# One core: x loaded turned for the router, and all condition matrices by one gather, turned by TensorE

## Chip, cores and metric

The kernel runs on one core of a Trainium2 chip. The metric is the device time of one execution in microseconds (us); the time before is the median of three runs.

## What is computed

x has 32 samples of 64 channels and 512 columns. Each sample is multiplied by one of 200 condition matrices (64 x 64), chosen by its index; the result has 2,048 tokens of 512. A router takes the softmax over 8 experts, and each token's best two. Each expert takes at most 640 assignments in order of tokens (CAP), and the outputs, weighted by the gates, are added to x.

```python
w = weights[conditions]
xc = jnp.einsum('bct,bcd->bdt', x, w)
logits = jnp.einsum('nh,eh->ne', xf, Wr)
gate = jax.nn.softmax(logits, axis=-1)
top2_val, top2_idx = jax.lax.top_k(gate, 2)
rank = (jnp.cumsum(onehot, axis=0) * onehot).sum(-1)
keep = rank <= cap
out_e = jnp.einsum('eni,ehi->enh', silu(g) * u, Wd)
y = jnp.einsum('ne,enh->nh', comb, out_e)
x = x + y
```

## The kernel before

Rows of x, 2,048 of 512, make 16 tiles of 128 rows (two samples each), handled as 8 pairs. The work is written out by hand for each engine, and semaphores order it. It has a front, which conditions and routes, and then the eight experts one after another.

**Router.** The router does not wait for the conditioned rows: it multiplies x by Wr first, and the small product by the condition matrix afterwards. For that TensorE turns each tile of x (x_tile_turn, L1169, four 128x128 turns into a bank of PSUM), ACT or DVE copies it to turned_sb (L600, L810), router(m) (L1180) multiplies, DVE copies the result to xrT (L817), turn(m) (L1193) turns it back and DVE sums it (L823). logits(g) (L1208) multiplies the pairs of group g by their matrices wq; top_two(g) (L826) takes the best two of each token. The groups LG are pairs 0 to 2, 3 and 4, 5 and 6, and 7.

**Condition matrices.** POOL gathers them by index (L446 to L456): for the first eight tiles by eight gathers of 64 rows for each sample straight to wq; for the last eight by one gather of rows of 2,048 bytes to wsel_sb, from which SP places them by eight transfers (place, L359).

**Conditioning.** condition(j) (L1225) multiplies a pair of tiles in eight matrix products of 64x64 by 512, in two rings of two banks; ACT copies each tile to xf_sb (xf_copy, L589) and SP writes each pair to xf_dram (L388 to L394).

**Routing.** From the one-hot matrix (L840) TensorE counts ranks (L1267), DVE works out the slots (L901 to L935) and TensorE puts them into lists (the slot matmuls, L1281), from which DVE makes src_row and dst_row (L950 to L966). TensorE then runs KEEP_WARM matmuls whose result nobody reads (L1287).

**Experts.** POOL gathers tiles of tokens from xf_dram by src_row (gather, L493); the first gather waits for src_row and for all of xf_dram (L484, L485). Weights are loaded by units: four of gate and up, one (KH) of down; for the three-product precision scheme, ACT rounds each unit to a high part (w_high, L604) and DVE takes the rest (w0_low, L937, for expert 0). Once the first gather has landed SP loads expert 1's units (L399 to L402), and, once five tiles have, copies x to out (L405 to L410), for which POOL waits at L568.

The steps on SP that order the front:

```python
            for m in range(NM - 1):
                sp.wait_ge(xf_ok, m * 2 + 2)
                sp.dma_start(xf_t[:, m * 2:m * 2 + 2, :],
                             xf_sb[:, m * 2:m * 2 + 2, :]).then_inc(xf_out, 16)
...
            sp.wait_ge(xg_in[0], 16)
            for u in range(NU):
                sp.wait_ge(wlo0_ok, u + 1)
                load_unit(1, u)
```

## Time and profile before

| what | value |
|---|---|
| runs | 274.13 us median (273.28 to 274.32) |
| the profiled execution | 271.69 us |
| its span, first to last instruction | 270.0 us |
| mean granted clock of TensorE | 0.99 |
| TensorE, DVE, ACT, POOL busy | 257.5, 161.8, 137.6, 171.2 us |
| moved by DMA | 59.00 MB, mean 219 GB/s |

A busy share is a mean over stages with different limits. The front ends at 41.62 us, when TensorE turns the first gathered tile of tokens; from there to the end TensorE has no long gaps. In the rows further down, L12 is line 12 of the kernel; a name with <- is the tile written and those read; xN counts instructions that are merged into one row.

### The profile page before, as it was taken

What the parts mean: (1) busy time and instruction counts of PE and PEld (TensorE: products, weight loads), DVE (VectorE), ACT (ScalarE), POOL (GpSimd) and SP (SyncE); (2) the same over time, 40 slices, a digit from 0 to 9 for tenths busy, and PEclk for the clock granted to TensorE, in tenths of its full rate; (3) what the DMA queues carried; (4) which work ended last, traced back from release to release, by engine and by line L of the source; (5) the groups of instructions that cost most, each with busy time, mean ns of one, the idle gap of its engine ahead of it and who ended that gap; (6) DMA issues with size and microseconds to landing.
All of it is one profiled execution on the core that took longest, in us unless ns stands there. A gap on an engine that the chain in (4) does not pass through costs nothing.

```text
span 270.0 us, 4016 instructions
## 1 busy us (share of the span) xinstructions
PE 257.5 (95%) x1368; PEld 199.9 (74%) x1368; DVE 161.8 (60%) x332; ACT 137.6 (51%) x242; POOL 171.2 (63%) x156
## 2 busy tenths in 40 slices
PE   8999798999999999999999999999999999999991
PEld 4563257999987867888878877887878777778980
DVE  2558997544459674776556638656773967243251
ACT  2356861444464655665376644666475368442100
POOL 5792047731158858875788387768876885585742
PEclk9999979999999999999999999999999999999998
DMA  6999848998879997899789867997899799366541
GB/s 203 364 305 342 358 165 266 382 330 312 298 221 214 203 253 197 138 253 276 178 143 231 245 189 124 241 322 174 171 266 298 127 182 216 41 79 81 146 164 45
DMA packets 27099, 59.00 MB, mean 219 GB/s; under 512 B 6198, under 2 KB 6454, under 8 KB 26976
## 3 DMA queue, kind: packets, MB, share of 16 engines
q1 hardware_dynamic: 16416, 37.89, 44.3%
q0 software_dynamic: 10656, 20.75, 37.2%
q8 instruction: 16, 0.26, 0.4%
q14 instruction: 11, 0.09, 0.1%
HBM read 39.56 MB, written 20.25 MB: 222 GB/s over the span
## 4 chain that ended last, share of the span: by engine, by line
PE 55%; DVE 18%; DMA 9%; ACT 8%; issue 6%; SPq 1%; ACTq 1%; POOLq 0%; DVEq 0%
PE bank L1340 16%; PE bank L1427 10%; PE bank L1314 10%; DMA xg<-xf_dram,src_turn 6%; PE bank L1435 5%; DVE w L996 4%; DVE squares L1045 4%; ACT hhi L695 3%; DMA x_sb<-x 3%; PE bank L1287 2%; PE bank L1301 2%; PE bank L1176 2%; DVE xlo L981 2%; ACT w L608 2%; DVE h L1111 1%
## 5 line engine op out<-in xcount | busy, mean ns | idle before, releaser
L1427 PE MATMUL bank<-xhi,w 128*128 128x512 f32 x280 | 71.5, 397 | 0.2 <-DVE h_last L1091 0.2
L1340 PE MATMUL bank<-w,hhi 128*128 128x512 f32 (+1 forms) x216 | 67.1, 392 | 1.1 <-DVE hlo L1051 1.1
L553 POOL DMA_INDIRECT out<-y_sb,dst_row x35 | 56.1, 1604 | 14.8 <-issue 10.4
L1427 PEld LDWEIGHTS bank<-xhi,w 128*128 128x128 f32 x280 | 52.5, 188 | 13.2 <-DVE h_last L1091 0.7
L519 POOL DMA_INDIRECT gate_g<-gates_dram,src_row x40 | 45.2, 1130 | 12.1 <-issue 10.5
L1340 PEld LDWEIGHTS bank<-w,hhi 128*128 128x128 f32 x216 | 39.2, 188 | 10.2 <-DVE hlo L1051 2.3
L996 DVE TENSOR_TENSOR w<-raw,w 128x704 fp32r<-128x704 f32 (+1 forms) x35 | 37.0, 1058 | 14.6 <-ACT w L608 8.2
L1340 PE MATMUL bank<-w,hlo 128*128 128x512 f32 (+1 forms) x108 | 42.0, 389 | 0.0
L507 POOL DMA_INDIRECT xg<-xf_dram,src_turn x24 | 25.5, 1063 | 26.1 <-DVE xlo L981 11.7
L1435 PE MATMUL bank<-xlo,w 128*128 128x512 f32 x140 | 38.4, 396 | 0.0
L608 ACT ACTIVATE w<-raw 128x704 fp32r<-128x704 f32 (+1 forms) x40 | 36.7, 922 | 0.0
L507 POOL DMA_INDIRECT xg<-xf_dram,src_row x16 | 17.6, 1102 | 27.9 <-DVE dst_row L965 15.7
L1045 DVE STREAM_TRANSPOSE squares<-xg 128x512 f32<-128x512 f32 x24 | 24.0, 1051 | 16.7 <-DMA xg<-xf_dram,src_turn 16.7
L1435 PEld LDWEIGHTS bank<-xlo,w 128*128 128x128 f32 x140 | 26.4, 188 | 6.4
L666 ACT ACTIVATE y_sb<-bank,gate_g 128x512 f32<-128x512 f32 x30 | 20.1, 685 | 20.0 <-PE bank L1340 18.7
L1340 PEld LDWEIGHTS bank<-w,hlo 128*128 128x128 f32 x108 | 20.3, 188 | 4.7
L1314 PE MATMUL bank<-w,xhi 128*128 128x352 f32 x112 | 20.5, 328 | 0.8 <-ACT xhi L643 0.8
L1314 PEld LDWEIGHTS bank<-w,xhi 128*128 128x128 f32 x112 | 18.2, 189 | 1.5 <-issue 1.0
L695 ACT ACTIVATE hhi<-h 128x512 fp32r<-128x512 f32 x14 | 8.8, 632 | 19.5 <-DVE h L1098 12.0
L1051 DVE TENSOR_TENSOR hlo<-h,hhi 128x512 fp32r<-128x512 f32 x14 | 9.7, 696 | 10.4 <-ACT hhi L695 10.4
L981 DVE TENSOR_TENSOR xlo<-xg,xhi 128x512 fp32r<-128x512 f32 x24 | 15.0, 685 | 0.2 <-ACT xhi L653 0.2
L653 ACT ACTIVATE xhi<-xg 128x512 fp32r<-128x512 f32 x24 | 13.2, 617 | 1.5 <-DMA xg<-squares 1.5
(138 smaller groups left out, 304.3 us busy)
## 6 DMA issues: line engine op xcount, KB each, us to landing
raw<-wgu SPq DMA_DIRECT2D x32, 352.0 KB, 7.7
xg<-squares SPq DMA_DIRECT2D x24, 256.0 KB, 7.1
x_sb<-x SPq DMA_DIRECT2D x8, 512.0 KB, 8.3
raw<-wd SPq DMA_DIRECT2D x8, 512.0 KB
xf_dram<-xf_sb SPq DMA_DIRECT2D x7, 512.0 KB, 3.7
raw<-wd SPq DMA_DIRECT2D x8, 192.0 KB
out<-x SPq DMA_DIRECT2D x1, 1280.0 KB, 17.9
gate_g<-gates_dram,src_row POOLq DMA_INDIRECT x40, 4.5
```

The lines of the kernel that those rows point to most:

```text
L507: nc.gpsimd.indirect_dma_start(out=xg[:, t, :], out_offset=None, in_=xf_dram[:, :], in_offset=bass.IndirectOffsetOnAxis(ap=rows, axis=0), ...
L519: nc.gpsimd.indirect_dma_start(out=gate_g[:, n % TPE, :], out_offset=None, in_=gates_dram[:, :], in_offset=bass.IndirectOffsetOnAxis(ap=sr ...
L553: nc.gpsimd.indirect_dma_start(out=out[:, :], in_=y_sb[:, n % TPE, :], in_offset=None, out_offset=bass.IndirectOffsetOnAxis(ap=dst_row[:, ...
L608: last = nc.scalar.activation(w[:, half, 0, a:b], raw[:, a:b], ACT.Copy)
L666: nc.scalar.activation(y_sb[:, t, :], y_bank(e, t)[:, :], ACT.Copy, scale=gate_g[:, t, e:e + 1]).then_inc(y_ok, n)
L981: nc.vector.tensor_tensor(xlo4[:, :, cols], turned_rows(e, t), xhi4[:, :, cols].bitcast(F32), ALU.subtract).then_inc(xlo_ok, n)
L996: last = nc.vector.tensor_tensor(w[:, half, 1, a:b], raw[:, a:b], w[:, half, 0, a:b].bitcast(F32), ALU.subtract)
L1045: nc.vector.transpose(squares[:, :, t, :], xg[:, t, :].rearrange("p (i b) -> p b i", i=SQ)).then_inc(squares_ok, 1)
L1314: last = nc.tensor.matmul(ps[:, 0:I], left[:, b, c], w[:, half, part, o:o + I], start=(k == 0 and left is xhi and part == 0), stop=(k == K ...
L1340: last = nc.tensor.matmul(ps[:, cols], left(c), w[:, half, part, o:o + width], start=(c == 0 and q == 0), stop=(closes and c == cs[-1] and ...
L1427: last = nc.tensor.matmul(ACC_BANK[what][:, :], columns(what, k, part), xhi4[:, k, :], start=(k == 0 and part == 0), stop=False)
L1435: last = nc.tensor.matmul(ACC_BANK[what][:, :], columns(what, k, 0), xlo4[:, k, :], start=False, stop=(k == KH - 1))
```

## The change

x comes from the host a second time, turned within each tile (xt), and is loaded in that form into x_sb, so that router(m) reads it straight from there and no tile is turned before the router. The conditioning still needs rows: for pairs 0 to 2 SP loads them over the turned ones once the router has read those (load_x_rows); for pairs 3 to 7 TensorE turns them back (turn_rows) and ACT copies them over the turned ones (rows_copy). The condition matrices come by one gather for all 32 samples: four partitions for each sample, 17 windows of 64 numbers (4,352 bytes) in each; TensorE turns overlapping pairs of windows (turn_matrices, ahead of router 4), and ACT and DVE copy them from four banks into wq. Conditions run in the order of CONDITIONED.

With it, three weight units of expert 0 are loaded ahead of the writes of xf_dram, the fourth behind them, and the down weights once the first gather has landed; their conversions move behind the conditioning, that of the down weights into the first expert. Exponentials and gates are taken once for all tiles. KEEP_WARM goes from 18 to 24. Below, removed lines are mostly left off; the functions above have them.

```diff
-PLACED = B // 2
-CQ = P // PLACED
-CP = C // CQ
+CQ = P // B
+DP = D // CQ
+WINDOWS = DP + 1
...
-BEFORE_RANKS = 4
-W0_EARLY = 1
+W0_EARLY = 3
+ROWS_LOADED = (0, 1, 2)
+ROWS_TURNED = (3, 4, 5, 6, 7)
+CONDITIONED = (3, 4, 0, 1, 2, 5, 6, 7)
...
-KEEP_WARM = 18
+KEEP_WARM = 24
...
+            def load_x_turned(m):
+                sp.dma_start(x_sb[:, m * 2:m * 2 + 2, :], xt[m, :, :, :]).then_inc(x_in[m], 16)
+            def load_x_rows(n):
+                m = ROWS_LOADED[n]
                 js = slice(m * 2, m * 2 + 2)
+                sp.wait_ge(xrT_ps, m + 1)
+                sp.dma_start(x_sb[:, js, :], x_t[:, js, :]).then_inc(rows_in[n], 16)
             sp.dma_start(condb[:, :], cond[:, :]).then_inc(cond_in, 16)
+            load_x_turned(0)
             sp.dma_start(wr_sb[:, :, :], wr[:, :, :]).then_inc(wr_in, 16)
+            for m in range(1, NM):
...
+                load_x_turned(m)
...
+            for n in range(len(ROWS_LOADED)):
+                load_x_rows(n)
...
+            for u in range(W0_EARLY):
                 load_unit(0, u)
+            for n, m in enumerate(CONDITIONED):
+                sp.wait_ge(xf_ok, n * 2 + 2)
                 sp.dma_start(xf_t[:, m * 2:m * 2 + 2, :],
                              xf_sb[:, m * 2:m * 2 + 2, :]).then_inc(xf_out, 16)
+            for u in range(W0_EARLY, KH):
+                load_unit(0, u)
+            sp.wait_ge(gates_ok, 1)
             sp.dma_start(gates_dram[0:N, :].rearrange("(p j) e -> p j e", j=TT),
                          gate[:, :, :]).then_inc(gates_out, 16)
             sp.wait_ge(xg_in[0], 16)
+            load_unit(0, KH)
...
-            for j in range(HALF):
-                nc.gpsimd.indirect_dma_start(
-                    out=wq[:, j, :], out_offset=None, in_=wcond[:, :],
-                    in_offset=bass.IndirectOffsetOnAxis(ap=cidx[:, j:j + 1], axis=0),
-                ).then_inc(row_in[group_of(j)], 16)
...
+            for b in range(XR):
+                act.wait_ge(wq_ps, b + 1)
+                nc.scalar.activation(wq_view(EVEN, b * XR, XR),
+                                     turned_matrices(b, EVEN, 0, 0, XR),
+                                     ACT.Copy).then_inc(wq_act_ok, 1)
+            def xf_copy(m, ring):
+                act.wait_ge(xf_ps, CONDITIONED.index(m) + 1)
+                for o in range(2):
+                    nc.scalar.activation(xf_sb[:, m * 2 + o, :], ps_xf[ring * 2 + o][:, :],
+                                         ACT.Copy).then_inc(xf_ok, 1)
+            def rows_copy(m, ring):
+                for o in range(2):
+                    act.wait_ge(turned_ps, ROWS_TURNED.index(m) * 2 + o + 1)
+                    nc.scalar.activation(x_sb[:, m * 2 + o, :], ps_xf[ring * 2 + o][:, :],
+                                         ACT.Copy).then_inc(turned_ok, 1)
...
+            rows_copy(3, 0)
+            rows_copy(4, 1)
+            xf_copy(3, 0)
+            xf_copy(4, 1)
+            rows_copy(5, 0)
+            rows_copy(6, 1)
+            xf_copy(0, 0)
+            xf_copy(1, 1)
+            rows_copy(7, 0)
+            xf_copy(2, 1)
+            xf_copy(5, 0)
+            xf_copy(6, 1)
+            xf_copy(7, 0)
+            exps()
...
+                if s == 0:
+                    w_high(KH, 0, 0)
...
+                if m == 4:
+                    for b in range(XR):
+                        dve.wait_ge(wq_ps, b + 1)
+                        n = XR if b < XR - 1 else XR - 1
+                        last = nc.vector.tensor_copy(wq_view(ODD, b * XR + 1, n),
+                                                     turned_matrices(b, ODD, 1, 0, n))
...
+                xrT_copy(m)
                 if m >= 1:
+                    xr_sum(m - 1)
+                if m in (5, 6):
+                    top_two(m - 5)
...
+            def turn_rows(m, ring):
+                for o in range(2):
+                    for k in range(KH):
+                        last = nc.tensor.transpose(ps_xf[ring * 2 + o][:, k * P:(k + 1) * P],
+                                                   xt_sb[:, m * 2 + o, k, :], ident[:, :])
+                    last.then_inc(turned_ps, 1)
...
+            def turn_matrices():
+                pe.wait_ge(wsel_in, 16)
+                for a in range(DP):
+                    last = nc.tensor.transpose(
+                        ps_xf[a // XR][:, a % XR * P:(a % XR + 1) * P],
+                        wsel_sb[:, a * C:(a + 2) * C],
+                        ident[:, :])
+                    if a % XR == XR - 1:
+                        last.then_inc(wq_ps, 1)
...
+                if m in ROWS_LOADED:
+                    pe.wait_ge(rows_in[ROWS_LOADED.index(m)], 16)
+                else:
+                    pe.wait_ge(turned_ok, ROWS_TURNED.index(m) * 2 + 2)
...
+            pe.wait_ge(wr_in, 16)
             for m in range(NM):
+                if m == 4:
+                    turn_matrices()
+                router(m)
                 if m >= 1:
+                    turn(m - 1)
+                if m == 5:
+                    pe.wait_ge(wq_act_ok, XR)
+                    pe.wait_ge(wq_dve_ok, XR)
+                    logits(0)
+                if m == 6:
+                    logits(1)
+                    turn_rows(3, 0)
+            turn_rows(4, 1)
             turn(NM - 1)
             logits(2)
             logits(3)
+            pe.wait_ge(turned_ok, 2)
+            condition(3, 0)
+            pe.wait_ge(turned_ok, 4)
+            condition(4, 1)
+            pe.wait_ge(xf_ok, 2)
+            turn_rows(5, 0)
+            pe.wait_ge(xf_ok, 4)
+            turn_rows(6, 1)
...
+            pe.wait_ge(turned_ok, 6)
+            condition(0, 0)
+            pe.wait_ge(turned_ok, 8)
+            condition(1, 1)
+            pe.wait_ge(xf_ok, 6)
+            turn_rows(7, 0)
+            pe.wait_ge(xf_ok, 8)
+            condition(2, 1)
+            pe.wait_ge(turned_ok, 10)
+            condition(5, 0)
+            pe.wait_ge(xf_ok, 10)
+            condition(6, 1)
+            pe.wait_ge(xf_ok, 12)
+            condition(7, 0)
...
+        "xt": np.asarray(x).reshape(NM, 2, P, KH, P).transpose(0, 4, 1, 3, 2).reshape(NM, P, 2, H),
...
+        "wcond": np.pad(np.asarray(L0_cond_weights).transpose(0, 2, 1).reshape(S * CQ, DP * C),
+                        ((0, 0), (0, C)), mode="wrap"),
```

Where the change moves instructions, these are the places that the prediction speaks of.

ACT, from its first copy on, before (turned_sb is the turned x, xf_sb the conditioned rows, w the rounded weights):

```order
L600 ACTIVATE turned_sb<-bank 128x512 [waits tT_ps] x2
L600 ACTIVATE turned_sb<-bank 128x512 [waits xrT_ps,tT_ps] x9
L592 ACTIVATE xf_sb<-bank 128x512 [waits xf_ps] x2
L619 ACTIVATE ex<-lg 128x80 [waits sub_ok]
L592 ACTIVATE xf_sb<-bank 128x512 [waits xf_ps] x2
L608 ACTIVATE w<-raw 128x704 [waits raw_in0]
L592 ACTIVATE xf_sb<-bank 128x512 [waits xf_ps] x2
L619 ACTIVATE ex<-lg 128x48 [waits sub_ok]
L592 ACTIVATE xf_sb<-bank 128x512 [waits xf_ps] x2
```

and now (wq are the condition matrices, x_sb the rows turned back):

```order
L592 ACTIVATE wq<-bank 64x64x4 [waits wq_ps] x4
L607 ACTIVATE x_sb<-bank 128x512 [waits turned_ps] x4
L600 ACTIVATE xf_sb<-bank 128x512 [waits xf_ps]
L600 ACTIVATE xf_sb<-bank 128x512
L600 ACTIVATE xf_sb<-bank 128x512 [waits xf_ps]
L600 ACTIVATE xf_sb<-bank 128x512
L607 ACTIVATE x_sb<-bank 128x512 [waits turned_ps] x4
L600 ACTIVATE xf_sb<-bank 128x512 [waits xf_ps]
L600 ACTIVATE xf_sb<-bank 128x512
L600 ACTIVATE xf_sb<-bank 128x512 [waits xf_ps]
L600 ACTIVATE xf_sb<-bank 128x512
L607 ACTIVATE x_sb<-bank 128x512 [waits turned_ps] x2
```

Eleven copies of turned x have gone from ahead of the conditioned rows; copies of rows, ten in all, now stand among them, and the weights and exponentials have moved behind.

TensorE around the middle of the router's pairs, before (L1176 turns x, L1188 is the router, L1199 turns its result):

```order
L1188 MATMUL bank_7<-turned_sb,wr_sb 32x256 [waits xrT_ok,tT_act_ok,tT_dve_ok]
L1188 MATMUL bank_7<-turned_sb,wr_sb 32x256 x3
L1199 MATMUL bank_7<-ident,xrT 128x128 [waits xr_ok,xrT_ok]
L1199 MATMUL bank_7<-ident,xrT 128x128
L1176 MATMUL bank<-ident,x_sb 128x128 [waits tT_dve_ok,x_in5]
L1176 MATMUL bank<-ident,x_sb 128x128 x3
L1176 MATMUL bank<-ident,x_sb 128x128 [waits tT_act_ok,x_in5]
L1176 MATMUL bank<-ident,x_sb 128x128 x3
```

and now (L1201 turns the condition matrices, L1157 is the router, L1177 turns its result):

```order
L1177 MATMUL bank_7<-ident,xrT 128x128 [waits xr_ok,xrT_ok]
L1177 MATMUL bank_7<-ident,xrT 128x128
L1201 MATMUL bank<-ident,xf_sb 128x128 [waits wsel_in]
L1201 MATMUL bank<-ident,xf_sb 128x128 x15
L1157 MATMUL bank_7<-x_sb,wr_sb 32x256 [waits xrT_ok,x_in4]
L1157 MATMUL bank_7<-x_sb,wr_sb 32x256 x3
L1177 MATMUL bank_7<-ident,xrT 128x128 [waits xr_ok,xrT_ok]
L1177 MATMUL bank_7<-ident,xrT 128x128
L1157 MATMUL bank_7<-x_sb,wr_sb 32x256 [waits xrT_ok,x_in5]
```

The turns of x ahead of each router are gone, and all turns of matrices stand in one place ahead of router 4, behind a wait for the one gather.

TensorE around the ranks, before (L1232 is the conditioning, L1267 and L1270 the ranks):

```order
L1232 MATMUL bank<-x_sb,wq 64x512 [waits xf_ok]
L1232 MATMUL bank<-x_sb,wq 64x512 x3
L1232 MATMUL bank<-x_sb,wq 64x512 [waits xf_ok]
L1232 MATMUL bank<-x_sb,wq 64x512 x3
L1267 MATMUL bank_7<-ohp,ones 128x264 [waits oh_clear,oh_ok,consts]
L1270 MATMUL bank_7<-ohp,upper 128x128
L1270 MATMUL bank_7<-ohp,upper_odd 128x128
L1232 MATMUL bank<-x_sb,wq 64x512 [waits xf_ok]
L1232 MATMUL bank<-x_sb,wq 64x512 x3
L1232 MATMUL bank<-x_sb,wq 64x512 [waits xf_ok]
L1232 MATMUL bank<-x_sb,wq 64x512 x3
L1232 MATMUL bank<-x_sb,wq 64x512 [waits xf_ok]
```

and now (L1217 is the conditioning, L1167 turns rows back, L1257 and L1260 the ranks):

```order
L1217 MATMUL bank<-x_sb,wq 64x512 [waits turned_ok]
L1217 MATMUL bank<-x_sb,wq 64x512 x3
L1217 MATMUL bank<-x_sb,wq 64x512 [waits turned_ok]
L1217 MATMUL bank<-x_sb,wq 64x512 x3
L1167 MATMUL bank<-ident,x_sb 128x128 [waits xf_ok]
L1167 MATMUL bank<-ident,x_sb 128x128 x7
L1167 MATMUL bank<-ident,x_sb 128x128 [waits xf_ok]
L1167 MATMUL bank<-ident,x_sb 128x128 x7
L1257 MATMUL bank_7<-ohp,ones 128x264 [waits oh_clear,oh_ok,consts]
L1260 MATMUL bank_7<-ohp,upper 128x128
L1260 MATMUL bank_7<-ohp,upper_odd 128x128
L1217 MATMUL bank<-x_sb,wq 64x512 [waits rows_in0,turned_ok]
```

Turns of two pairs, each behind a wait for ACT's copies, have come between the first conditions and the ranks.

## Rows read from the trace of the kernel before

**Rows 1.** The chain of waits, 10 to 45 us (start us, us, what)
```profile
3.22 7.35 DMA x_sb<-x
...
12.65 0.87 PE bank L1176 x8
13.52 0.57 PE bank L1188 x8
14.09 0.37 PE bank L1199 x2
...
33.43 2.55 PE bank L1281 x32
35.98 5.58 PE bank L1287 x18
...
41.62 0.64 PE bank L1301 x4
```

**Rows 2.** ACT in order of time, 31 to 50 us (start, busy, instructions [idle before])
```profile
31.11 2.06 ACT L592 ACTIVATE xf_sb<-bank 128x512 f32 x4 [0.32 <-PE bank L1232]
...
36.64 1.47 ACT L608 ACTIVATE w<-raw 128x1536 fp32r<-128x1536 f32 x1
...
47.61 0.46 ACT L677 ACTIVATE g_sb<-bank 128x352 f32<-128x352 f32 x1 [1.25 <-PE bank L1314]
49.88 0.49 ACT L683 ACTIVATE hhi<-bank 128x384 fp32r<-128x384 f32 x1 [1.80 <-PE bank L1368]
```

**Rows 3.** SP's transfers: the last writes of xf_dram, and the first placing one
```profile
10.87 5.14 SPq L361 DMA_DIRECT2D wq<-xf_sb  x8
...
32.71 1.32 SPq L394 DMA_DIRECT2D xf_dram<-xf_sb  x2
```

**Rows 4.** Transfers issued at 32.0 to 32.6 us (size, us from issue to landing)
```profile
xf_dram<-xf_sb SPq DMA_DIRECT2D x1, 512.0 KB, 3.2
```

**Rows 5.** The same, issued at 33.1 to 34 us
```profile
xf_dram<-xf_sb SPq DMA_DIRECT2D x1, 256.0 KB, 3.5
```

**Rows 6.** POOL in order of time: first gather of matrices, first gather of tokens
```profile
3.38 1.14 POOL L446 DMA_INDIRECT xf_sb<-wcond,cidx  x1 [1.72 <-DVE cidx L792]
...
37.46 1.55 POOL L507 DMA_INDIRECT xg<-xf_dram,src_row  x1 [15.70 <-DVE dst_row L965]
```

**Rows 7.** Transfer queues in 8 to 9 us (packets, MB, share of 16 engines)
```profile
q0 software_dynamic: 21, 0.09, 23.6%
```

**Rows 8.** DVE in order of time, 14 to 20 us
```profile
15.97 0.42 DVE L817 COPY xrT<-bank 128x256 f32<-128x256 f32 x1 [1.25 <-PE bank L1188]
...
18.61 0.54 DVE L831 MAX8 v<-bank 128x8 f32<-128x8 f32 x6 [0.27 <-PE bank L1221]
...
19.96 0.16 DVE L834 FIND_INDEX8 i<-v,bank 128x8 uint32<-128x8 f32 x1
```

**Rows 9.** PE in order of time, 18 to 32 us
```profile
18.01 0.53 PE L1221 MATMUL bank<-xr,wq 64*64 64x8 f32 x24
...
20.69 1.07 PE L1232 MATMUL bank<-x_sb,wq 64*64 64x512 f32 x8
...
27.05 0.27 PE L1267 MATMUL bank<-ohp,ones 128*128 128x264 bf16 x1 [0.49 <-issue]
...
29.86 2.07 PE L1232 MATMUL bank<-x_sb,wq 64*64 64x512 f32 x16 [0.44 <-ACT xf_sb L592]
```

**Rows 10.** Stretches: busy us (instructions) of PE, PEld, DVE, ACT, POOL; PEclk, DMA share, GB/s
```profile
4.00:12.00 8.00, 7.45 (x63) 4.57 (x60) 3.57 (x7) 2.05 (x4) 6.17 (x7) 1.00 1.01 353
32.00:36.00 4.00, 2.57 (x33) 2.52 (x34) 3.96 (x7) 3.98 (x7) 0.00 (x0) 1.00 1.00 392
36.00:39.00 3.00, 3.00 (x8) 1.03 (x7) 2.88 (x11) 2.10 (x3) 1.54 (x1) 0.50 0.10 25
```

**Rows 11.** POOL in order of time: the gathers behind the initial copy to out
```profile
72.41 1.00 POOL L507 DMA_INDIRECT xg<-xf_dram,src_turn  x1 [6.88 <-DMA out<-x]
76.07 1.00 POOL L507 DMA_INDIRECT xg<-xf_dram,src_turn  x1 [2.66 <-PE bank L1301]
```

More of the change, by code:

```diff
@@ L271, in build @@
         xf_t = xf_dram[0:N, :].rearrange("(p j) h -> p j h", j=TT)
-        TURN_DVE = [1, 2, 5, 6, 9]
-        TURN_ACT = [j for j in range(TT) if j not in TURN_DVE]
         def group_of(j):
@@ L1272, in _ @@
             last.then_inc(rank_ps, 1)
-            for j in range(after, TT, 2):
-                condition(j)
+            pe.wait_ge(turned_ok, 6)
[12 more added lines that the diff above has]
+            condition(7, 0)
             pe.wait_ge(consts, CONSTS)
```

222 lines of the change are left out of this document (61 added, 161 removed).

## The prediction

> **What bounds the kernel now.** I read the chain of waits first, then each engine in order of time up to 45 us, then the transfers, and last the places further on where a moved transfer could be late. From 41.62 us on the chain is TensorE at work on the first expert; the change touches little behind that point. So the question is when the first gathered tile of tokens can be turned, 41.62 now [rows 1]. Two things end just there: 18 warming matmuls end at 41.56 [rows 1], and the first gather, issued at 37.46 [rows 6], lands. The gather waits for the token list and for all writes of xf_dram. The slot matmuls that make the list end at 33.43 + 2.55 = 35.98 [rows 1]. ACT's last copy of conditioned rows ends at 31.11 + 2.06 = 33.17 [rows 2]; the last write is the second of a pair of issues that begins at 32.71 and takes 1.32, so issued at about 33.2 [rows 3], and lands 3.5 later, at 36.7 [rows 5]. That is later than the list, and the gather's start follows it by 0.76. The row names dst_row, for which this gather does not wait; the writes were what came last. **The bound of this stage is therefore: ACT's copies, the last write, the gather.** A write of a whole pair, issued half a microsecond before, took 3.2 [rows 4], as long as a half: no queue of transfers stood in front of them. They wait for ACT.
>
> **What is removed.** 64 TensorE turns of x, 0.87 us for each pair [rows 1], and their 16 copies on ACT and DVE go from ahead of the router. Eight small gathers on POOL and eight placing transfers go too. None of that is a gain by itself: the router needs x, and pair 3 lands at 3.22 + 7.35 = 10.57 [rows 1]; transfer engines stand at a share of 1.01 from 4 to 12 us [rows 10]. The cover of the removed work, the arrival of x, stays.
>
> **What is added ahead of the logits: one gather that all of them wait for.** Now the gather is issued from 3.38 to 4.52 [rows 6], has 0.09 MB moved in 8 to 9 us [rows 7], and the first placing transfer, which waits for it, starts at 10.87 [rows 3]. It moves 128 rows of 2,048 bytes, 0.26 MB; the new one moves 128 rows of 17 x 64 x 4 = 4,352 bytes, 0.56 MB. Lower bound 10.8 (size is hidden), upper bound 15 (it comes behind all of x). I take 11.5: nearest is today's gather, and 0.30 MB more at 392 GB/s [rows 10] is 0.75. The Trainium skill, "DMA: Bandwidth & Descriptors", section "Queues, rings and completion order", has each transfer engine take turns between queues, a packet at a time; by that the gather would wait for one pair of x at most, and its landing would lie at the lower bound, 0.7 us less in the sum. The 0.09 MB that it moved in 8 to 9 us beside x [rows 7] agree with the turns; that it is still at work 3.5 us after its issue ended does not.
>
> In order from 11.5: 16 turns of matrices at 0.87 / 8 = 0.109 [rows 1], 13.3; router of pair 4, 0.57 [rows 1]; DVE's last matrix copy and the copy of the router's result, each as the 256-column copy, 0.42 [rows 8], 14.5; router of pair 5, 0.57, 15.0; a turn, 0.37 [rows 1], 15.4; the first logits, 0.5 [rows 9], 15.9. Then DVE's first top two, 18.61 to 20.12 now, 1.5 [rows 8]: 17.6 with hand-overs. The second logits wait for it, and TensorE's first rows to be turned back stand behind those: **18.0**. x is not later: pair 4 would need 0.5 MB more than pair 3, at 353 GB/s [rows 10] 1.5 us, and the new gather's 0.56 MB another 1.6, so 13.7 at worst against the 13.3 at which its router is wanted; I take nothing for it.
>
> **What is added behind: ten more copies on ACT, in one line with the sixteen it has.** Turning back five pairs gives TensorE 40 turns, 4.4 us, and ACT 10 copies. ACT then has 26 copies of 512 columns; four take 2.06 now [rows 2], 0.49 each behind one another: 12.7. The first can start 0.6 after its turns do (four at 0.109 and the hand-over). In two rings of two banks each copy also frees the bank of TensorE's next step, so the two engines take turns. A condition takes TensorE 1.07 [rows 9], and today's copies start 31.11 - 29.86 = 1.25 behind a start of conditions [rows 2, 9]. Written out step by step this leaves ACT idle five times: 0.85 while TensorE runs router 7 and a turn ahead of the next rows; 1.4 while it runs the last turn, two logits and the first condition; 0.7 behind the rank matmuls; 0.4 twice behind late conditions: 3.7. Sum 18.0 + 0.6 + 12.7 + 3.7 + 0.1 = **35.1**, against 33.17.
>
> The last write is a whole pair: issued 35.15, 3.3 to land (between the 3.2 and 3.5 of now), 38.45 against 36.7. **The first gather starts 1.8 later**, at 39.2, and lands near 43.3. The list is not what ends: the last condition starts when pair 5 is copied, 32.85, ends at 33.8, slot matmuls of 2.55 and 0.25 make 36.6, under the write by 1.9. The rank matmuls, at 27.05 now [rows 9], come at about 25.8; this gain is spent waiting for TensorE's conditions. 24 warming matmuls at 5.58 / 18 = 0.31 [rows 1] would end at 43.8, with the higher clock throughout at 41.5 (7 of them fill 36 to 39 us at 0.50 [rows 10], 0.43 each, and half of that is 0.21): 0 to 0.5, I take 0.
>
> **Transfers that are moved.** SP's three reloads of x rows (1.6 MB) and three weight units (1.1 MB) go between x and the writes: 2.7 MB at 392 GB/s are 6.9 us from about 15, done by 22; the first write comes at about 24. Covered, and rows for pairs 0 to 2 are wanted only at 26. Weight unit 3 goes behind the writes, wanted first behind the gather: nothing. The down weights are loaded once the first tile lands; their conversion, 1.47 on ACT [rows 2], goes between the first SiLU, ending 47.61 + 0.46 = 48.07, and the copy at 49.88 [rows 2]: it fits the 1.8 of idle time with 0.3 left, if the load is there in 6.5 us. Price 0 to 0.5; I take 0. On SP expert 1's down weights now hold up the initial copy to out. POOL's wait for that ends at 72.41, the next gather waits for TensorE until 76.07 [rows 11]: 2.4 us to spare against 1.2 of waiting and 0.7 MB, 1.9 us, of transfer. Price 0 to 0.7; I take 0.
>
> **Sum.** +1.8 us. The profiled execution took 271.69 (span 270.0), so 273.5 for it; it lies 2.4 under the median of the runs, 274.13, which becomes **275.9**. Each microsecond by which the matrices land later moves the end by one.
>
> **Rivals.**
> *TensorE falls to 1.2 GHz.* From router 3, at about 9.5, until the matrices land it has nothing to do for 2 us, and before that only the routers and turns, 0.94 for each pair. Now it is at 1.00 from 4 to 12 with 7.45 of 8 us busy; it was granted 0.50 in 36 to 39, behind a stretch with 2.57 of 4 us busy [rows 10]. At half the clock the 16 turns take 3.5 instead of 1.74: 1.75 and a little more, **277.8**. The Trainium skill, "TensorE: Matmul & The Clock Gate", section "HAM oscillation — how this bites in real kernels", says that bursts between waits for transfers run at the lower clock; the drop at 36 [rows 10] agrees. Against it: the wait may be shorter than that.
> *The matrices come behind x.* At 15 it is +5.3, **279.4**. For it: 6.3 us now from the end of the issue to the placing transfer [rows 3, 6]; against it: the gather moves among x's packets now [rows 7], and pair 3 lands beside it.
> *The matrices come early,* by 11 or before. +0.2 to +1.3, **274.9**; below about 10 the pairs of x set the pace. For it: today's landing. Against it: over twice the bytes. The Trainium skill's page "DMA: Bandwidth & Descriptors" would have it so.
> *The other side: faster, because the list ends the stage.* If ACT's five idle stretches close up (TensorE's steps ready ahead of each copy), copies end by 31.4, the writes land at 34.8 and the list decides. The ranks come 1.25 earlier; from there to the slot matmuls it is 33.43 - 27.05 = 6.4 [rows 1, 9], so list at 25.8 + 6.4 + 2.55 + 0.25 = 35.0, and the gather 0.3 later: -2.2, **271.9**. It decides from the point where ACT ends before 31.6. For it: ACT and TensorE have two rings. Against it: the order puts logits, ranks and router 7 between the two halves, whatever the speed.
>
> **How the numbers follow.** Forecast as worked out, landing of the matrices 11 to 13: 0.40. Lower clock: 0.20. Behind x: 0.05. Early: 0.24. List ends the stage: 0.11. The forecast's own range is 275.4 to 277.4. The range 273.2 to 279.0 reaches over the early and the clock case, leaving out most of the faster case and the last. 0.5%, 1.37 us, is what a measurement here can tell. Slower: forecast, clock and late gather, 0.65, less the forecast's lower edge, 0.62; same: the early case and that edge, 0.26; faster 0.12.
>
> **What would show it.** Right: ACT's last copy of xf_sb near 35, first gather near 39, 26 copies with five gaps; matrix turns at 11 to 12. Wrong in the sum: matrix turns elsewhere, or 0.21 each. Wrong in kind: the first gather starts right behind src_row instead of behind the last write, or the first expert waits for the down weights.

## The result, and the profile after

The changed kernel takes 281.19 us at the median of four runs (278.89 to 281.63); the kernel before, beside it, 274.09 (273.28 to 274.32). The ratio is 1.0248, interval 1.0187 to 1.0308. (Ratios leave out the executions far above the fastest of a kernel; medians here are of all.) So it is slower by 7.1 us, where the prediction said 1.8 and put the end of its range at 279.0. The profiled execution took 280.85, span 279.0: 9.0 more than the span before. The forecast for a profiled execution was 273.5, so the profile is 7.4 off.

The chain of waits of the changed kernel, from the last write on (start us, us, what), answers to [rows 1] and [rows 6]:

```profile
37.87 3.62 DMA xf_dram<-xf_sb
...
42.27 4.05 DMA xg<-xf_dram,src_row
...
46.45 1.03 PE bank L1303 x4
...
48.25 3.86 PE bank L1316 x12
...
82.38 1.46 PE bank L1303 x12
```

The stage is bound by what the prediction named: ACT's copies, the last write, the first gather. But the gather starts 4.81 later than before, not 1.8, and the first tile is turned at 46.45 instead of 41.62. Behind that point more is lost: the last turns of the gathered tokens of expert 1 (the second of the eight, counted from 0) end at 83.84, 37.39 behind the first turn; before they ended at 76.17, 34.55 behind it. This distance is the second mark below.

TensorE of the changed kernel in order of time (start, busy, line [idle before]):

```profile
7.68 0.64 PE L1157 MATMUL bank<-x_sb,wr_sb 128*32 128x256 f32 x8 [1.39 <-DMA x_sb<-xt]
...
8.96 1.08 PE L1157 MATMUL bank<-x_sb,wr_sb 128*32 128x256 f32 x8 [0.27 <-DMA x_sb<-xt]
...
11.25 1.08 PE L1157 MATMUL bank<-x_sb,wr_sb 128*32 128x256 f32 x8 [0.59 <-DMA x_sb<-xt]
...
12.75 3.42 PE L1201 MATMUL bank<-ident,xf_sb 128*128 128x128 f32 x16
...
20.83 1.09 PE L1167 MATMUL bank<-ident,x_sb 128*128 128x128 f32 x8
...
39.02 5.36 PE L1289 MATMUL bank<-iota_q 128*128 128x512 f16 x24
46.45 1.02 PE L1303 MATMUL bank<-ident,xg 128*128 128x128 f32 x4 [2.07 <-DMA xg<-xf_dram,src_row]
```

A router takes 1.08 instead of 0.64, the sixteen turns of matrices 3.42 (1.97 at the full clock, in late_warm further down), and the warming matmuls end 2.07 us before the tile is there. The stretches, with the columns of [rows 10], say why:

```profile
4.00:12.00 8.00, 5.75 (x41) 1.51 (x38) 1.64 (x5) 0.00 (x0) 7.51 (x15) 0.81 0.93 355
9.00:15.00 6.00, 5.41 (x31) 3.39 (x32) 2.04 (x6) 0.68 (x2) 2.85 (x4) 0.50 1.03 417
...
47.00:53.00 6.00, 5.22 (x20) 4.78 (x19) 4.14 (x17) 0.60 (x1) 4.89 (x6) 0.50 0.92 274
```

TensorE was granted 0.50, that is 1.2 of its 2.4 GHz, from 9.0 to 15.8 us, behind a stretch in which it waited for x (1.39 and 0.27 us), and from 46.55 to 53.4, behind the 2.07 us of idle time. The kernel before had one such stretch ahead of its last microseconds, 36.0 to 39.4 [rows 10], which fell on its warming matmuls. Three of the change's four runs have a mean granted clock of 0.969 or 0.970 and spans of 279.0 to 279.8; the fourth has 0.989 and 277.2.

### The profile page after: what moved, and what is told of

The parts are those of the page before. It is cut to its first block, busy times and chain, and to the rows that moved or that the text cites. A ratio compares the mean times of both kernels' runs of the same rounds, so it can differ in the third digit from the quotient of the medians.

```text
span 279.0 us, 3954 instructions
## 1 busy us (share of the span) xinstructions
PE 262.8 (94%) x1366; PEld 203.3 (73%) x1366; DVE 159.6 (57%) x326; ACT 137.9 (49%) x244; POOL 167.9 (60%) x148
## 3 DMA queue, kind: packets, MB, share of 16 engines
HBM read 41.16 MB, written 20.25 MB: 220 GB/s over the span
## 4 chain that ended last, share of the span: by engine, by line
PE 53%; DVE 15%; DMA 13%; ACT 8%; issue 8%; SPq 1%; POOLq 1%; ACTq 0%; DVEq 0%; POOL 0%
PE bank L1342 13%; PE bank L1431 12%; PE bank L1316 10%; DMA xg<-xf_dram,src_turn 8%; PE bank L1439 6%; DVE w L984 4%; DVE squares L1035 3%; DMA x_sb<-xt 3%; ACT hhi L700 2%; PE bank L1303 2%; DVE xlo L969 2%; ACT xf_sb L600 2%; PE bank L1167 2%; PE bank L1217 2%; DMA xg<-xf_dram,src_row 1%
## 5 line engine op out<-in xcount | busy, mean ns | idle before, releaser
L554 POOL DMA_INDIRECT out<-y_sb,dst_row x35 | 56.8, 1623 | 12.6 <-issue 10.4
L520 POOL DMA_INDIRECT gate_g<-gates_dram,src_row x40 | 47.3, 1182 | 12.1 <-issue 10.8
L508 POOL DMA_INDIRECT xg<-xf_dram,src_row x16 | 19.6, 1223 | 44.5 <-DMA xf_dram<-xf_sb 30.4
L1316 PE MATMUL bank<-w,xhi 128*128 128x352 f32 x112 | 22.0, 344 | 0.8 <-ACT xhi L646 0.8
L1316 PEld LDWEIGHTS bank<-w,xhi 128*128 128x128 f32 x112 | 19.6, 202 | 1.6 <-issue 1.1
L1041 DVE TENSOR_TENSOR hlo<-h,hhi 128x512 fp32r<-128x512 f32 x14 | 9.7, 692 | 10.8 <-ACT hhi L700 10.8
```

What stands on the lines that cost most here:

```text
L508: nc.gpsimd.indirect_dma_start(out=xg[:, t, :], out_offset=None, in_=xf_dram[:, :], in_offset=bass.IndirectOffsetOnAxis(ap=rows, axis=0), ...
L520: nc.gpsimd.indirect_dma_start(out=gate_g[:, n % TPE, :], out_offset=None, in_=gates_dram[:, :], in_offset=bass.IndirectOffsetOnAxis(ap=sr ...
L554: nc.gpsimd.indirect_dma_start(out=out[:, :], in_=y_sb[:, n % TPE, :], in_offset=None, out_offset=bass.IndirectOffsetOnAxis(ap=dst_row[:, ...
L1316: last = nc.tensor.matmul(ps[:, 0:I], left[:, b, c], w[:, half, part, o:o + I], start=(k == 0 and left is xhi and part == 0), stop=(k == K ...
```

## The experiments

Two marks are compared for each kernel, from its profile: the start of the first gather and of the first x turn (TensorE turning the first gathered tile), and the distance from that turn to the end of expert 1's last x turns. The runs come from several rounds; each ratio is to the kernel before as it ran in the same round (medians 273.2 to 274.2), so ratios compare better between rows than medians do.

| kernel | median us | ratio to before [interval] | first gather | first x turn | distance |
|---|---|---|---|---|---|
| before | 274.09 | | 37.46 | 41.62 | 34.55 |
| the change | 281.19 | 1.0248 [1.0187, 1.0308] | 42.27 | 46.45 | 37.39 |
| late_warm | 280.23 | 1.0267 [1.0217, 1.0318] | 40.70 | 44.74 | 36.44 |
| early_warm | 281.32 | 1.0260 [1.0172, 1.0349] | 40.36 | 44.47 | 36.08 |
| both_warm | 279.50 | 1.0236 [1.0173, 1.0300] | 41.11 | 44.93 | 36.53 |
| before_cold | 274.75 | 1.0060 [1.0020, 1.0099] | 37.31 | 40.96 | 37.27 |
| lw_out_first | 278.33 | 1.0212 [1.0159, 1.0265] | 43.17 | 47.18 | 35.27 |
| lw_early_down | 278.41 | 1.0152 [1.0083, 1.0221] | 42.15 | 46.28 | 34.48 |
| before_late_down | 273.35 | 1.0002 [0.9967, 1.0037] | 37.63 | 41.82 | 34.95 |
| lw_rows_five | 278.33 | 1.0172 [1.0094, 1.0250] | 38.11 | 42.50 | 36.27 |
| three_fixes | 278.28 | 1.0175 [1.0138, 1.0211] | 41.12 | 44.76 | 37.40 |
| old_matrices | 284.95 | 1.0438 [1.0388, 1.0489] | 48.26 | 52.36 | 36.35 |
| both_out_first | 277.16 | 1.0114 [1.0071, 1.0157] | 41.16 | 44.99 | 34.52 |
| rows_five_mended | 276.45 | 1.0102 [1.0066, 1.0139] | 38.97 | 43.03 | 36.07 |

### The clock: late_warm, early_warm, both_warm, before_cold

late_warm and, on the kernel before, before_cold:

```diff
-KEEP_WARM = 24
+KEEP_WARM = 32
...
-KEEP_WARM = 18
+KEEP_WARM = 8
```

early_warm (both_warm has it together with the 32):

```diff
                 if m >= 1:
                     turn(m - 1)
+                for _ in range((5, 1, 5)[m] if m < 3 else 0):
+                    nc.tensor.matmul(bank[4], warm[:, 0:P], warm[:, :], start=True, stop=True)
```

> The changed kernel with 32 warming matmuls behind the slot matmuls in place of 24; nothing else. In the profile of the change the 24 ran 39.02 to 44.38 (0.22 each), TensorE stood idle 2.07 us until the gathered tile landed at 46.45, and it was granted 0.50 of its clock from 46.55 to 53.37. Clock theory: 32 end at about 46.2, so the idle time goes, the first expert runs at 1.00, its first 24 steps of L1316 take 3.9 instead of 4.1 and the 12 before them 2.2 instead of 3.9; the x turn stays at 46.4, the first turn of h comes about 2.7 earlier, and the run ends 2.3 to 2.8 us earlier (about 278.5 by the median, 278.1 for the profile). Transfer theory (the first expert waits for its weights or its rows whatever the clock): the clock is 1.00 but the end moves by less than 1 us.

> The changed kernel with 11 idle matmuls more on TensorE ahead of the logits: 5 behind router 0, 1 behind router 1, 5 behind router 2, 0.21 us each, where it waits for x (1.39, 0.27 and 0.59 us idle in the profile of the change, the last two already at 0.50). Clock theory: 1.00 throughout the first 36 us; the matrix turns start at about 12.2 and take 1.8 instead of 3.4, rows of pair 3 are turned from about 18.5 instead of 20.8, the last copy of ACT ends near 35.5 instead of 37.9 and the first gather starts near 40.0 instead of 42.3; the warming matmuls end earlier too, so the second drop of the clock stays, and the end moves by 2.0 to 2.4 us (about 278.9 by the median). Rival, the matrices set the stage: they land at about 12.7 in any case, the turns start there and the gain is 1.7 or less. Rival, the copies set the pace: the first gather moves by less than 0.7.

> Both edits: 11 idle matmuls ahead of the logits and 32 warming matmuls behind the slot matmuls. Clock theory: the gains add, 4.5 to 5.1 us against the change (about 276.4 by the median), so that the loss against the kernel before shrinks from 7 to about 2.3, which is near the sum of the prediction without a drop of the clock (+1.8). If they do not add, the earlier gather meets another bound (the token list, or transfers that stand in front of it), and the gather's landing shows it.

> The kernel before with 8 warming matmuls in place of 18: everything else as it was. There they run from 35.98, the first eight at 0.43 us, and end at 41.56, just as the gathered tile lands. With 8 they end at about 39.4 and TensorE is idle for 2.2 us. Clock theory: the first expert then runs at half the clock here too, for some 7 us, and the kernel before loses 2.3 to 2.8 us by that alone (about 276.7 by the median), the same price as in the change. Rival: if the clock comes back before the tile lands, or the first expert waits for its weights in any case, it loses under 1 us.

The late drop of the clock went away in the profile of late_warm as expected, and the time did not follow. TensorE of late_warm:

```profile
11.41 0.64 PE L1157 MATMUL bank<-x_sb,wr_sb 128*32 128x256 f32 x8 [1.25 <-DMA x_sb<-xt]
...
12.59 1.97 PE L1201 MATMUL bank<-ident,xf_sb 128*128 128x128 f32 x16 [0.17 <-DMA xf_sb<-wcond,cidx]
...
19.22 1.09 PE L1167 MATMUL bank<-ident,x_sb 128*128 128x128 f32 x8
...
44.74 0.63 PE L1303 MATMUL bank<-ident,xg 128*128 128x128 f32 x4 [0.25 <-DMA xg<-xf_dram,src_row]
...
79.19 0.66 PE L1303 MATMUL bank<-ident,xg 128*128 128x128 f32 x4 [0.80 <-DMA xg<-xf_dram,src_row]
80.55 0.63 PE L1303 MATMUL bank<-ident,xg 128*128 128x128 f32 x4 [0.70 <-DMA xg<-xf_dram,src_row]
```

The clock is 1.00 up to the last microseconds, the turns of matrices take 1.97, and the first rows are turned back 1.61 earlier than in the change. (This execution happened to have no early drop, though nothing was done about it: the same steps of TensorE ahead of the matrices fell to 0.50 in the profiles of the change, lw_out_first and lw_early_down, and not in late_warm and lw_rows_five. Of the six profiled kernels with the idle matmuls none fell up to 16 us. The profiled execution took 278.28 at a mean clock of 0.994; late_warm's other three runs, 279.76 to 280.71, have 0.980 to 0.985, and no profile shows where they lost it.) But TensorE now waits ahead of expert 1's last x turns, where the change hardly did: the last tiles are late, as the last two lines show. The chain has one gather there:

```profile
60.88 19.54 DMA xg<-xf_dram,src_row
```

So the distance shrank by 0.95 only, and the ratio did not move. Half the clock in the first expert and this late gather cover each other. In the change the same gather, the fourth for expert 1, started at 65.34, took 17.7 and landed at 83.0, so the last turn, which ends at 83.84, came right behind it there too: TensorE reached it just as it landed. (The other order, the gather mended and the clock left, was not run.)

early_warm moved the front by 2.0, as expected (first turn 44.47), left the late drop, and got a new one, 108 to 112 us, behind a wait of 2.9 us in expert 1:

```profile
44.47 0.63 PE L1305 MATMUL bank<-ident,xg 128*128 128x128 f32 x4 [2.05 <-DMA xg<-xf_dram,src_row]
...
46.00:50.00 4.00, 4.00 (x18) 3.93 (x19) 3.80 (x17) 0.17 (x1) 3.27 (x4) 0.61 0.95 308
108.00:112.00 4.00, 4.00 (x12) 3.13 (x11) 0.86 (x1) 1.33 (x3) 3.28 (x3) 0.57 0.79 261
```

both_warm kept 1.00 until the last microseconds and was still only 1.7 faster than the change at the median, with the ratio unmoved; 4.5 to 5.1 had been expected. It too has a late gather for expert 1, 19.50 us from 61.19 on, and TensorE waits for it.

before_cold prices the late drop by itself. TensorE of that kernel, then a stretch of it:

```profile
35.91 2.85 PE L1287 MATMUL bank<-iota_q 128*128 128x512 f16 x8
40.96 0.80 PE L1301 MATMUL bank<-ident,xg 128*128 128x128 f32 x4 [2.20 <-DMA xg<-xf_dram,src_row]
...
40.00:48.00 8.00, 6.26 (x24) 5.86 (x25) 5.73 (x18) 1.19 (x2) 6.47 (x6) 0.58 0.88 285
```

2.20 us of idle time, half the clock from 41.2 to 48.1, and a distance of 37.27 instead of 34.55: **2.7 us**, as expected. The run lost 1.6 us by the ratio (0.5 to 2.7), somewhat less than that.

### What waits behind: lw_out_first, lw_early_down, before_late_down

lw_out_first (SP; 32 warming matmuls, as in the next one):

```diff
-            for u in range(NU):
+            for u in range(KH):
                 sp.wait_ge(wlo0_ok, u + 1)
                 load_unit(1, u)
...
             sp.dma_start(out[N:N + CAP, :], x[0:CAP, :]).then_inc(out_init, 16)
+            sp.wait_ge(wlo0_ok, NU)
+            load_unit(1, KH)
```

lw_early_down; before_late_down is the same edit the other way round, on the kernel before:

```diff
-            for u in range(W0_EARLY):
+            for u in (*range(W0_EARLY), KH):
                 load_unit(0, u)
...
-            load_unit(0, KH)
...
+            w_high(KH, 0, 0)
             x_high(0)
...
-                if s == 0:
-                    w_high(KH, 0, 0)
...
-                if s == 0:
-                    w0_low(KH)
...
+            w0_low(KH)
             x_low(0)
```

> late_warm (the change with 32 warming matmuls) with one move on SP: the initial copy of x to out is issued ahead of expert 1's down weights and no longer behind them. In late_warm the last gather of the first expert's tiles had been issued at 46.8, the copy was issued at 55.45 (in the kernel before 51.17, 9.55 behind the first x turn; in late_warm 10.7), and expert 1's gather of 60.88 took 19.5 us beside it; TensorE waited for it at the last two x turns, which ended at 81.18, 36.4 behind its first x turn against 34.55 in the kernel before. Transfer theory (the down weights that the change loads late hold up the copy, and expert 1's gathers are slow beside the copy): the copy is issued near 51 to 52, the last x turn of expert 1 ends 34.6 behind the first (79.3 for a first turn at 44.7), and the run is 1.5 to 2.5 us faster than late_warm, near 278 by the median. Rival (the gather is slow for the bytes alone, whatever the order): the last x turn still ends 36 or more behind the first, and the time stays within 0.7 of late_warm.

> late_warm with the first expert's down weights loaded as in the kernel before: behind the first three weight units and ahead of the writes of xf_dram, converted ahead of the first x turn and no longer behind the first SiLU. It undoes one part of the change, the late load. Transfer theory: the initial copy to out is issued 9.5 to 10 us behind the first x turn, the last x turn of expert 1 ends about 34.6 behind the first, and the run is 1.5 to 2.5 us faster than late_warm; the price may be a first write that takes longer (0.7 MB more ahead of it), which the first gather would show as a start later than 40.7. Rival (the copies of ACT are all that counts): within 0.7 of late_warm.

> The kernel before with that one part of the change alone: the first expert's down weights loaded behind its first gather instead of ahead of the writes, and converted behind the first SiLU. Transfer theory: the front stays (first x turn at about 41.6), the initial copy to out is issued 1 to 4 us later than 51.2, the last x turn of expert 1 ends 1 to 2.5 later than 76.2, and the run is 1 to 2.5 us slower than the kernel before (274.5 to 276). Rival (hidden, as the prediction took it): within 0.7 of the kernel before.

Both edits took the distance back, to 35.27 and 34.48, and both were faster than late_warm by 1.8 to 1.9 at the median, as the transfer theory had it (the intervals of the ratios still overlap late_warm's). SP of late_warm and then of lw_out_first shows the turn-about:

```profile
54.79 0.47 SPq L387 DMA_DIRECT2D raw<-wd  x1
55.45 2.46 SPq L416 DMA_DIRECT2D out<-x  x4
```

```profile
56.32 2.48 SPq L416 DMA_DIRECT2D out<-x  x4
...
59.81 0.58 SPq L384 DMA_DIRECT2D raw<-wd  x1
```

The copy is issued 10.7 and 9.1 us behind the first x turn; in the kernel before it was 9.55 (51.17), in the change 13.5 (59.91), so there the half clock had held it up further. The profiles of both new kernels had the early drop again, with first turns at 47.18 and 46.28; their late clock was 1.00. On the kernel before, though, the same late load cost nothing: 1.0002. There the copy is issued 10.7 behind the first turn too, a gather takes 18.02, and TensorE waits for the last tile, but the distance grows by 0.4 only:

```profile
57.98 18.02 DMA xg<-xf_dram,src_row
76.14 0.63 PE bank L1304 x4
```

So the load's place alone does not cost the time; the expectation of 1 to 2.5 us for this run failed. A slow gather is no cause by itself either; what goes with the distance is when it lands. POOL's issue of expert 1's fourth gather and its time to landing, in the kernel before and then in the change:

```profile
57.80 1.00 POOL L507 DMA_INDIRECT xg<-xf_dram,src_row  x1 [2.47 <-PE bank L1301]
...
xg<-xf_dram,src_row POOLq DMA_INDIRECT x1, 16.9
...
65.34 1.00 POOL L508 DMA_INDIRECT xg<-xf_dram,src_row  x1 [4.37 <-PE bank L1303]
...
xg<-xf_dram,src_row POOLq DMA_INDIRECT x1, 17.7
```

It lands 23.5 and 23.1 us behind the copy's issue, and 22.2 to 25.4 in all fourteen profiles. Behind the first turn that is 33.1 in the kernel before, 34.2 in before_late_down, 35.7 in late_warm and 36.6 in the change; where TensorE waits for it, the last turn ends 0.8 later. The kernel before had about 0.7 us of slack there, which took in most of its own late load. Why it lands 1.5 later in late_warm than in before_late_down, with the copy issued equally late, is not shown.

### The two halves of the change: lw_rows_five, old_matrices

lw_rows_five, with the orders of ACT and TensorE rewritten to match (ACT: 0, 1, 2, turned 5, 3, turned 6, 4, turned 7, 5, 6, 7); 32 warming matmuls:

```diff
-ROWS_LOADED = (0, 1, 2)
-ROWS_TURNED = (3, 4, 5, 6, 7)
-CONDITIONED = (3, 4, 0, 1, 2, 5, 6, 7)
+ROWS_LOADED = (0, 1, 2, 3, 4)
+ROWS_TURNED = (5, 6, 7)
+CONDITIONED = (0, 1, 2, 3, 4, 5, 6, 7)
```

old_matrices (with 32 warming matmuls, and idle ones ahead of the logits), cut to its core:

```diff
+            sp.wait_ge(wsel_in, 16)
+            for j in range(HALF, TT):
+                place(j)
...
+            for j in range(HALF):
+                nc.gpsimd.indirect_dma_start(
+                    out=wq[:, j, :], out_offset=None, in_=wcond[:, :],
+                    in_offset=bass.IndirectOffsetOnAxis(ap=cidx[:, j:j + 1], axis=0),
+                ).then_inc(row_in[group_of(j)], 16)
...
-                if m == 4:
-                    turn_matrices()
```

> late_warm with five pairs loaded as rows (0 to 4) and three turned back (5 to 7), where the change has three and five; the conditions run in order of the pairs, and those of pairs 0 and 1 start ahead of and behind the second logits. ACT has 22 copies of 512 columns in one line in place of 26, SP two loads of 0.5 MB more. Copy theory (ACT's line of copies sets the last write, 16.3 us from 19.9 to 36.2 in late_warm): ACT's first copy near 19.5 to 20, four copies less and fewer idle gaps, last copy at 33.5 to 34.5, first gather 1.7 to 2.7 us earlier than 40.70, and the run 1.5 to 2.5 us faster than late_warm. Rival (transfers set the last write: two loads more stand in front of it): rows land late, ACT waits for conditions that wait for rows, and the first gather moves by less than 1 us or comes later.

> The change with its matrix part undone: matrices by nine gathers and eight placing transfers as in the kernel before, no turns of matrices and none of their copies; x turned, three pairs as rows and five turned back stay. 32 warming matmuls, 13 idle ones ahead of the logits. Matrix theory (what the front lost beyond the prediction without a drop of the clock is the one gather, landing at about 12.4, and 1.9 us of turns): router 4 at 12 to 13 where the next pair of x lands, rows of pair 3 turned from 17 to 17.6 instead of 19.3, the last copy of ACT 1.7 to 2.3 earlier than the 36.3 of both_warm, first x turn near 42.9. Rival (x itself arrives late, or the second logits wait for placed matrices): rows of pair 3 from 18.5 or later.

lw_rows_five confirms that ACT's line of copies sets the front. Its ACT, against the line from 19.91 to 36.23 in late_warm:

```profile
19.03 1.08 ACT L600 ACTIVATE xf_sb<-bank 128x512 f32<-128x512 f32 x2 [4.30 <-PE bank L1215]
20.39 1.08 ACT L600 ACTIVATE xf_sb<-bank 128x512 f32<-128x512 f32 x2 [0.27 <-PE bank L1215]
23.73 1.08 ACT L600 ACTIVATE xf_sb<-bank 128x512 f32<-128x512 f32 x2 [2.25 <-PE bank L1215]
...
32.98 1.10 ACT L600 ACTIVATE xf_sb<-bank 128x512 f32<-128x512 f32 x2 [0.23 <-PE bank L1215]
```

Four copies less, last copy at 34.08, first gather 2.6 earlier, in spite of 1 MB more to load: here the transfers do not set the last write. The first turn then comes, without idle time, right behind the 32 warming matmuls. Its runs lie wide apart, 274.10 to 281.55, with mean clocks of 0.995 and 0.978 at the two ends, and the profile is of the 274.10.

old_matrices missed its aim. TensorE there, then SP:

```profile
23.78 0.61 PE L1191 MATMUL bank<-xr,wq 64*64 64x8 f32 x16 [5.80 <-DMA wq<-xf_sb]
```

```profile
11.50 6.55 SPq L367 DMA_DIRECT2D wq<-xf_sb  x8
```

The placing transfers, issued behind the three loads of rows on the same queue, land only at about 23.7, and the second logits wait 5.8 us. So it is no price of the new matrix part. It shows that with rows reloaded early, the old way of placing matrices does not fit in this order.

### The sum: three_fixes, both_out_first, rows_five_mended

three_fixes is both_warm with the down weights early; both_out_first is both_warm with the copy ahead; rows_five_mended adds to lw_rows_five:

```diff
-KEEP_WARM = 32
+KEEP_WARM = 21
...
                     condition(1, 1)
+                    pe.wait_ge(xf_ok, 2)
+                    condition(2, 0)
+            pe.wait_ge(xf_ok, 4)
+            turn_rows(5, 1)
             turn(NM - 1)
             logits(2)
             logits(3)
-            pe.wait_ge(xf_ok, 2)
-            condition(2, 0)
-            pe.wait_ge(xf_ok, 4)
-            turn_rows(5, 1)
```

and the edits of early_warm and lw_out_first.

> The change with the three mends together: 11 idle matmuls ahead of the logits (as in early_warm), 32 warming matmuls (late_warm), the first expert's down weights early (lw_early_down). The design stays: turned x, one gather of matrices, three pairs loaded as rows and five turned back. If the clock and the held copy to out are all that the prediction left out, there is no stretch at 0.50 before the last 6 us, the first x turn comes at 44.5 to 45, expert 1's last turn 34.5 to 35 behind it, and the run is 3 to 4 us slower than the kernel before (276.3 to 277.5 by a median of 273.2 for it). Rival: if more is lost in the experts behind the first, whatever the start, it stays above 278.

> both_warm (11 idle matmuls ahead of the logits, 32 warming matmuls) with the copy to out issued ahead of expert 1's down weights, as in lw_out_first; the first expert's own down weights stay late, so that nothing stands ahead of the conversion of its fourth unit (in three_fixes that unit landed 6.0 us after its issue at 36.59, the down weights' conversion came behind it, and TensorE waited 1.5 us inside the first expert). If the clock, the held copy and that wait are what lies between the forecast and the measurement, the first x turn comes at 44.5 to 45, TensorE is at 1.00 until the last 6 us, expert 1's last turn ends 34.6 to 35.3 behind the first, and the run is 3 to 4.3 us slower than the kernel before (276.3 to 277.6 for 273.3). Rival (the experts behind the first are slower in any case): above 278.

> The version that the runs point to: five pairs as rows and three turned back as in lw_rows_five, the condition of pair 2 ahead of router 7 and the first rows turned back ahead of the last logits (ACT waited 2.25 us for that condition there), 11 idle matmuls ahead of the logits, 21 warming matmuls, the copy to out issued ahead of expert 1's down weights. Copy theory: ACT's last copy near 32.9 instead of 34.06, the list near 37.2 (36.0 there), first gather near 37.5 as in the kernel before, first x turn at 41.3 to 42, expert 1's last turn about 35 behind it: the run within 1.5 us of the kernel before, either way. Rival (transfers are now the bound): the last write takes over 4 us to land, the first gather stays at 38 or later and the run is 2 us or more slower.

three_fixes met a new wait, as its chain shows:

```profile
36.59 6.01 DMA raw<-wgu
42.62 0.79 ACT w L613
...
44.92 1.38 ACT w L613
46.33 1.76 DVE w L930
48.09 0.61 DVE xlo L960
48.74 1.44 PE bank L1315 x4
```

The fourth weight unit, issued behind the last write, lands late, and the down weights' conversion stands behind it: on ACT ahead of the high part of the first tile, for which TensorE idles 1.54 us, and on DVE ahead of its low part, 0.29 more. From 48.5 to 52 TensorE was granted 0.55.

both_out_first leaves that conversion late, and its profile is as expected; TensorE, and POOL's gather behind the copy:

```profile
12.82 1.97 PE L1203 MATMUL bank<-ident,xf_sb 128*128 128x128 f32 x16 [0.24 <-DMA xf_sb<-wcond,cidx]
...
44.99 0.63 PE L1307 MATMUL bank<-ident,xg 128*128 128x128 f32 x4 [0.27 <-DMA xg<-xf_dram,src_row]
...
78.04 1.47 PE L1307 MATMUL bank<-ident,xg 128*128 128x128 f32 x12
```

```profile
76.01 1.00 POOL L510 DMA_INDIRECT xg<-xf_dram,src_turn  x1 [7.14 <-DMA out<-x]
```

No drop before 271 us, distance 34.52 as in the kernel before, first turn 3.4 later: the median is 277.16 against 274.18, **3.0 us**, ratio 1.0114 [1.0071, 1.0157], whose interval lies below those of the change and of both_warm. So with the clock and the copy mended the design costs about 3 us; the other 4 of the change's 7 are what these edits took away. rows_five_mended comes as near in ratio, and no nearer: ACT's last copy ended at 34.9, not 32.9, the first gather started at 38.97, not 37.5, and its 21 warming matmuls ended 1.92 us before the tile, with 0.57 of the clock from 44.5 to 48.5 behind that. No version here beats the kernel before.

## Why the prediction was wrong

Right: the direction; that the stage ends with ACT's copies, the last write and the gather. ACT's line of 26 copies and five gaps was put at 16.5 us (18.6 to 35.1) and took 16.3 (21.52 to 37.85, and the same in late_warm). That its parts add up so well is luck: the five gaps were 0.72, 1.12, 0.60, 0.27 and 0.23, 2.9 and not 3.7, and the copies took 13.4 and not 12.7, since four in 2.06 are 0.515 each, not 0.49. The list was hidden: src_row at 39.24, the last write landed at 41.49. The late down weights of the first expert made nobody wait in the first expert.

Wrong, in the order of the prediction's own sum:

- **Start of the matrix turns, taken at 11.5 from the landing of the matrices.** Without a drop they began at 12.35 (lw_rows_five), 12.59 (late_warm) and 12.82 (both_out_first). That is 1.1 us of the sum, inside the bounds of 10.8 and 15 that the prediction gave, and by its own rule the end moves by the same. But the matrices were not what took most of it: TensorE waited for them 0.53, 0.17 and 0.24 us, and in both_warm not at all. Ahead of them in its order stand router 3 and a turn, which began at 10.82, 11.41 and 11.57, when pair 3 of x had landed. The prediction took nothing for x and set router 3 at about 9.5, against its own row of 10.57 for that landing; an early landing of the matrices would have gained 0.5 at most. The last write took 3.7 and 3.9 in late_warm and both_out_first, not 3.3: 0.4 to 0.6 more. With both, the forecast of 43.3 for the first turn becomes 44.8 (late_warm) and 45.2 (both_out_first); measured were 44.74 and 44.99.
- **The rival "TensorE falls to 1.2 GHz", with a chance of 0.20.** Its mechanism and its price held: 1.75 and a little more forecast; the first turn is 1.7 later in the profile of the change than in late_warm, and 1.5 and 2.4 later in the two others that fell. It fell in three of five profiles of this instruction stream, too few to set a chance by, but 0.20 looks low. I had set its start at the wait for the matrices; it fell earlier, behind the waits for pairs 1 and 2 of x. The drop of the kernel before that I set beside it came behind a wait of 1.50 us for DVE, not for a transfer.
- **The warming matmuls, "0 to 0.5, I take 0".** This step failed in kind. I asked only when they would end, 41.5 with the higher clock, against a tile at 43.3, and took an early end as free. At the full clock 24 of them take 5.36, the idle time behind them took the clock away, and the first expert paid 2.7 (before_cold). The row for it stood in [rows 10]: half the clock behind 2.57 of 4 us busy. The Trainium skill, "TensorE: Matmul & The Clock Gate", section "HAM oscillation — how this bites in real kernels", tells the same of a burst that starts behind a wait for a transfer; the runs here agree, with a shorter wait than in its example (2.07 us, behind 5.36 us of matmuls), and I had used it for the first wait alone.
- **The copy to out, "0 to 0.7, I take 0".** This step took the wrong waiter. I asked for POOL's gather behind the copy [rows 11]. That still had slack: in late_warm and in the change POOL waited last for TensorE there. What came late were expert 1's own gathers, which run beside the copy, the fourth landing 22 to 25 us behind its issue. In late_warm the copy is issued 1.2 later behind the first turn than before, which is what I had worked out, and in the change 3.9 later, since the half clock holds it up too (in before_cold that alone made 1.4). The distance falls by 2.0 when the copy goes ahead (both_warm 36.53, both_out_first 34.52).

These last two are not added: each hides the other. From the first turn to the end of expert 1's turns the change loses 2.84, both_warm still 2.0 without any drop. By the medians the clock alone gave back 1.7 (both_warm) and its ratio nothing that can be told apart; with the copy moved it is 4.0.

In the profile the miss adds up: the first turn is 3.15 later than forecast (46.45 for 43.3), the distance 2.84 longer, and what follows 1.37 longer, together 7.4. The median missed by less, 5.3, by luck: the profile of the kernel before lay 2.4 under its median, as the prediction said, and the forecast carried that over, but the change's lay only 0.3 under its own.

Left open: how often the early drop comes, since only profiles show where the clock fell; the mean clocks alone do not. And the experts behind expert 1, the same code in all kernels: from the end of its turns to TensorE's last instruction it is 187.84 before, 187.46 in before_cold, 188.93 in before_late_down, 187.64 in lw_rows_five, 189.21 in the change, 189.19 in both_out_first, 190.40 in both_warm, and 192.95 in early_warm with its drop at 108 us. I take that as the scatter of their gathers, but no run was made for it, so up to 2.6 us of a single profile stay unexplained.

## What to carry to other kernels

Warming matmuls that end early are not free: ask what TensorE does in the microseconds behind the last of them, and size them by the landing of what they wait for, at the full clock. When a gain from one fix does not show, look at what ends last next; two causes of about equal size cover each other, and only the run with both mended tells the sum. A transfer that is moved behind a wait holds up everything that the same engine issues behind it, and what suffers may be a third transfer that merely runs beside that.

## What the runs showed that I had not expected

- The same steps of TensorE fell to half the clock in some executions and kept it in others: the change had 0.81 from 4 to 12 us, late_warm 1.00.
- Work did not bring the clock back at once: in the change it stayed at 0.50 from 47 to 53 us with 5.22 of 6 us busy.
- The first gather of a tile took 4 us (4.05 in the change), the fourth for expert 1, beside the initial copy to out, 16.9 in the kernel before and 19.5 in late_warm. That it is slow did not matter; when it landed did.
